# Cross-attention and FFN layer on one core: value product around the scores, input turned by VectorE through HBM, mask added on VectorE

## The reference, cut to what matters

```
xl    = layernorm(x)
q,k,v = xl @ Wq, ctx @ Wk, ctx @ Wv              # 512 -> 32 heads of 128
score = q.k / sqrt(128) + position_bias          # 16 x 32 x 64 x 64
score = where(mask, score, -inf); probs = softmax(score), 0 where not mask
x     = x + (probs @ v) @ Wo
out   = x + base(layernorm(x)) + lora(layernorm(x), router)
```

## Time and profile before

| | us |
|---|---|
| median of 3 runs | 779.62 |
| the runs | 779.62, 779.64, 775.87 |
| the profiled execution, its own time | 777.37 |
| span in its profile (first to last instruction) | 775.5 |
| PE busy | 766.0 |
| DVE busy | 541.8 |
| ACT busy | 384.8 |
| POOL busy | 196.6 |

### The profile page before, as it was taken

How to read it: one execution, slowest core, us unless ns; L and a number is a source line. 1 busy time by engine, 2 the same in 40 slices (tenths; PEclk the granted TensorE clock), 3 DMA queues, 4 the chain that set the end, 5 groups by cost and what they waited for, 6 DMA issues and landing times.

```text
span 775.5 us, 16682 instructions
## 1 busy us (share of the span) xinstructions
PE 766.0 (99%) x6272; PEld 639.1 (82%) x6272; DVE 541.8 (70%) x979; ACT 384.8 (50%) x1110; POOL 196.6 (25%) x203
## 2 busy tenths in 40 slices
PE   9999999999999999999999999999999999999998
PEld 7888888888888888887888888888888888888886
DVE  5874626257677676578778877887678767867974
ACT  5662526245555464475654465435543565426510
POOL 0224041014424433323132312232122313010300
PEclk9999999999999999999999999999999999999999
DMA  6536673244565456577766777556756666541002
GB/s 231 203 123 217 220 244 137 109 140 160 163 190 164 164 163 187 167 235 217 229 181 209 226 208 208 170 176 205 201 165 197 201 188 196 154 148 57 1 15 95
DMA packets 128236, 133.05 MB, mean 172 GB/s; under 512 B 46479, under 2 KB 93583, under 8 KB 128158
## 3 DMA queue, kind: packets, MB, share of 16 engines
q1 hardware_dynamic: 128158, 132.00, 54.3%
HBM read 88.98 MB, written 42.99 MB: 170 GB/s over the span
## 4 chain that ended last, share of the span: by engine, by line
PE 94%; DVE 3%; issue 1%; ACT 1%; DMA 0%; ACTq 0%
PE pY L1452 43%; PE pP L1452 40%; PE pY L1613 4%; PE pO L1649 2%; PE pT_ L1649 1%; PE pO L1452 1%; DVE y L1167 1%; ACT pr L798 1%; PE pS L1649 1%; DVE st L1018 1%; PE pO L1501 0%; PE pS L1501 0%; DVE wk_lo L948 0%; PE pY L1528 0%; DVE wo_lo L948 0%
## 5 line engine op out<-in xcount | busy, mean ns | idle before, releaser
L798 ACT ACTIVATE pr<-pr,mx 128x64 f32<-128x64 f32 x256 | 86.2, 343 | 68.0 <-DVE mx L1187 68.0
L1452 PE MATMUL pY<-wo_hi,oT_hi 128*128 128x512 f32 x248 | 97.3, 392 | 0.3 <-DVE y L1167 0.2
L1452 PE MATMUL pY<-wo_lo,oT_hi 128*128 128x512 f32 x248 | 96.6, 389 | 0.0
L1452 PE MATMUL pY<-wo_hi,oT_lo 128*128 128x512 f32 x248 | 96.5, 389 | 0.0
L1167 DVE TENSOR_TENSOR y<-y,pY 128x512 f32<-128x512 f32 x124 | 83.9, 676 | 15.2 <-PE pY L1452 14.1
L690 ACT CAST wk_hi<-twk 128x256 fp32r<-128x256 f32 x128 | 50.7, 408 | 65.2 <-PE pP L1452 53.4
L948 DVE TENSOR_TENSOR wk_lo<-wk_raw,wk_hi 128x256 fp32r<-128x256 f32 x96 | 48.5, 506 | 46.5 <-ACT wk_hi L690 45.1
L1452 PE MATMUL pP<-xo_hi,wk_hi 128*128 128x512 f32 x196 | 77.9, 398 | 0.0
L1452 PE MATMUL pP<-xo_lo,wk_hi 128*128 128x512 f32 x196 | 76.4, 390 | 0.0
L1452 PE MATMUL pP<-xo_hi,wk_lo 128*128 128x512 f32 x196 | 76.4, 390 | 0.0
L623 POOL TENSOR_TENSOR bias<-bias,madd 128x512 f32<-128x512 f32 x32 | 41.3, 1306 | 137.6 <-DMA bias<-in_fside_Bx32xSxS 137.5
(11 more groups left out here) (283 smaller groups left out, 1862.2 us busy)
## 6 DMA issues: line engine op xcount, KB each, us to landing
v_hbm<-stage SPq DMA_DIRECT2D x64, 256.0 KB, 2.1
k_hbm<-stage SPq DMA_DIRECT2D x64, 256.0 KB, 3.7
k<-k_hbm SPq DMA_DIRECT2D x16, 1024.0 KB, 6.4
v<-v_hbm SPq DMA_DIRECT2D x16, 1024.0 KB, 7.2
wk_raw<-in_L_xattn_Wk SPq DMA_DIRECT2D x16, 512.0 KB, 4.6
wo_raw<-in_L_xattn_Wo SPq DMA_DIRECT2D x16, 512.0 KB, 3.7
bias<-in_fside_Bx32xSxS SPq DMA_DIRECT2D x128, 64.0 KB, 3.6
wk_raw<-in_L_xattn_Wq SPq DMA_DIRECT2D x16, 512.0 KB, 4.6
```

Of the source, the lines that this page charges most:

```text
L798: nc.scalar.activation(pr[s][:, b, :], pr[s][:, b, :], ACT.Exp, bias=mx[:, s, b:b + 1], accum_out=sm[:, s, b:b + 1]).then_inc(exp_made, 1)
L1452: mm = nc.tensor.matmul(bank_, a, b, start=first and n == 0, stop=last and n == len(terms) - 1, skip_group_check=read_between)
```

## The change

The mask is no longer added to the bias by GpSimd; DVE adds it to the biased scores, as one more instruction between `biased` and `largest`. In the loop `times_v` of the first head goes ahead of both scores, and that of the second stays behind them. PE no longer turns x: DVE turns it in 32x32 blocks, SP writes each tile to HBM and reads it back across partitions in four DMAs (`x_out`, `x_back`), and ACT and DVE read the turned x from SBUF instead of PSUM; `rows_out` is not called for it. The moments and the normalising of x come one block earlier.

```diff
-FIRST_TURN = [0, 1, 4, 6, 8, 10, 12, 14]
+FIRST_TURN = [0, 1, 4, 6]
+            def x_out(j):
+                for i in range(2):
+                    sp.wait_ge(xb_made, 2 * j + i + 1)
+                    sp.dma_start(x_hbm[2 * j + i], xb[:, i, :, :].rearrange("p a n -> p (a n)")).then_inc(put_x[i], 16)
+            def x_back(j):
+                if j >= 1:
+                    sp.wait_ge(sum_step, 4 * (4 + j))
...
+                for i, dst in enumerate((first_x, low[1])):
+                    sp.wait_ge(put_x[i], 16 * (j + 1))
+                    blocks = x_hbm[2 * j + i].rearrange("(t k) (a n) -> a k t n", t=4, a=4)
+                    for a in range(4):
+                        sp.dma_start(dst[32 * a:32 * a + 32, :, :], blocks[a]).then_inc(ld_xt[i], 16)
...
                     load_wk(n - 10)
+                if 17 <= n < 29 and n % 3 == 2:
+                    x_out((n - 17) // 3)
                 if n != Q0:
                     store(n, 0, c11_made)
                 if 0 < n:
                     store(n - 1, 2, c21_made)
+                if 17 <= n < 29 and n % 3 == 2:
+                    x_back((n - 17) // 3)
...
-            def add_mask(h):
-                pool.wait_ge(ld_bias[h % 2], 64 * (h // 2 + 1))
-                b = bias[h % 2]
-                nc.gpsimd.tensor_tensor(b[:, :, :], b[:, :, :], madd[:, :, :], ALU.add).then_inc(bias_made, 1)
...
-                act.wait_ge(turned, FIRST_TURN[j] + 1)
+                if j < 4:
+                    act.wait_ge(turned, FIRST_TURN[j] + 1)
+                else:
+                    act.wait_ge(ld_xt[0], 64 * (j - 3))
...
+                for i in range(2):
+                    m = 2 * n + i
+                    dve.wait_ge(xn_made, m + 1)
+                    if n >= 1:
+                        dve.wait_ge(put_x[i], 16 * n)
+                    nc.vector.transpose(xb[:, i, :, :].rearrange("p g (c q) -> p c g q", c=DC),
+                                        xn[:, i, :].rearrange("p (c g q) -> p c g q", c=DC, g=4)).then_inc(xb_made, 1)
...
                 dve.wait_ge(s_full, h + 1)
-                dve.wait_ge(bias_made, h + 1)
+                dve.wait_ge(ld_bias[h % 2], 64 * (h // 2 + 1))
...
+                dve.wait_ge(s_read, h + 1)
+                dve.wait_ge(mask_made, 1)
+                nc.vector.tensor_tensor(pr[h % 2][:, :, :], pr[h % 2][:, :, :], madd[:, :, :], ALU.add
+                                        ).then_inc(masked, 1)
             def largest(h):
-                dve.wait_ge(s_read, h + 1)
+                dve.wait_ge(masked, h + 1)
...
-                if prep_at(n) is not None:
-                    turn_pair(prep_at(n))
...
                 if i == 0:
                     turn_p(h)
                     turn_p(h + 1)
-                scores(h + 2)
-                scores(h + 3)
-                times_v(h)
+                    scores(h + 2)
+                    scores(h + 3)
+                    times_v(h)
+                    times(n, 2)
+                else:
+                    times_v(h)
+                    scores(h + 2)
+                    scores(h + 3)
                 times_v(h + 1)
-                for p in (1, 2, 6, 7) if i else (2, 6, 7):
+                for p in (1, 2, 6, 7) if i else (6, 7):
                     times(n, p)
...
             h = 2 * i
+            times_v(h)
             scores(h + 2)
-            times_v(h)
             times_v(h + 1)
             scores(h + 3)
             ffn_weights(0)
```

More of the change, by code:

```diff
@@ L351, in raw_block, with first_of, second_of, like @@
             return raw[:, 2 * r:2 * r + 2, c * width:(c + 1) * width]
+        def first_of(j):
+            if j < 4:
+                return first_turn(j)[:, :].rearrange("p (c t) -> p c t", c=DC)
+            return first_x[:, :, :].rearrange("p t (c q) -> p c t q", c=DC)
+        def second_of(j):
+            if j < 4:
+                return second_turn(j)[:, :].rearrange("p (c t) -> p c t", c=DC)
+            return low[1][:, :, :].rearrange("p t (c q) -> p c t q", c=DC)
+        def like(j, a):
+            return a if j < 4 else a.rearrange("p c (t q) -> p c t q", t=4)
         def tw_of(w):
@@ L366, in tile_cols, with a01_of @@
             return slice(j % 4 * P, (j % 4 + 1) * P)
+        def a01_of(j, part):
+            return a_part(j, part)[:, 0:2, :, tile_cols(j)].rearrange("p k c t -> p (k c) t")
         def piece(n, i):
@@ L629, in _ @@
                     sums_of_b(wset(n + 1))
[L630 to L636, removed]
+                if 15 <= n < 27 and n % 3 == 0:
+                    rstd_of((n - 15) // 3 * 2)
+                    rstd_of((n - 15) // 3 * 2 + 1)
             for i in range(NP):
@@ L692, in first_high @@
             def first_high(j):
-                act.wait_ge(turned, FIRST_TURN[j] + 1)
-                nc.scalar.copy(a_part(j, 0)[:, 0:2, :, tile_cols(j)],
-                               first_turn(j)[:, :].rearrange("p (k c t) -> p k c t", k=2, c=2)).then_inc(a01_hi, 1)
+                if j < 4:
+                    act.wait_ge(turned, FIRST_TURN[j] + 1)
+                else:
+                    act.wait_ge(ld_xt[0], 64 * (j - 3))
+                nc.scalar.copy(like(j, a01_of(j, 0)), first_of(j)).then_inc(a01_hi, 1)
             def rows_out(j):
@@ L706, in last_high @@
             def last_high(j):
[L708 to L711, removed]
+                if j < 4:
+                    act.wait_ge(turned, SECOND_TURN[j] + 1)
+                else:
+                    act.wait_ge(ld_xt[1], 64 * (j - 3))
+                nc.scalar.copy(like(j, a_part(j, 0)[:, 6, :, tile_cols(j)]), second_of(j)[:, 2:4]).then_inc(a6_hi, 1)
             def sums_high(j):
@@ L778, in _ @@
                     first_high(j)
-                    rows_out(j)
                     last_high(j)
@@ L971, in first_low @@
             def first_low(j):
-                cols = tile_cols(j)
                 dve.wait_ge(a01_hi, j + 1)
-                lower(a_part(j, 1)[:, 0:2, :, cols], first_turn(j)[:, :].rearrange("p (k c t) -> p k c t", k=2, c=2),
-                      a_part(j, 0)[:, 0:2, :, cols], a01_lo)
+                lower(like(j, a01_of(j, 1)), first_of(j), like(j, a01_of(j, 0)), a01_lo)
             def last_low(j):
@@ L981, in last_low @@
                 dve.wait_ge(a6_hi, j + 1)
-                lower(a_part(j, 1)[:, 6, :, cols], second_turn(j)[:, 2 * P:4 * P].rearrange("p (c t) -> p c t", c=2),
-                      a_part(j, 0)[:, 6, :, cols], a6_lo)
+                lower(like(j, a_part(j, 1)[:, 6, :, cols]), second_of(j)[:, 2:4],
+                      like(j, a_part(j, 0)[:, 6, :, cols]), a6_lo)
             def sums_of_a(j):
-                low_, s, k = low[j // 4], sums_a[j // 4], SUM_ORDER.index(j)
-                one = first_turn(j)[:, :].rearrange("p (k c t) -> p k c t", k=2, c=2)
+                s, k = sums_a[j // 4], SUM_ORDER.index(j)
+                s2, s3, s1, s4 = (like(j, s[:, n, :, :]) for n in range(4))
                 if j == 0:
-                    one, low_ = kept0
+                    a11, a12 = kept0[0][:, 0, :, :], kept0[0][:, 1, :, :]
+                    rows_ = kept0[1][:, :, :]
                     dve.wait_ge(kept0_made, 2)
                 else:
-                    dve.wait_ge(low_made, k + 1 if j < 4 else k)
+                    a11, a12 = first_of(j)[:, 0:2], first_of(j)[:, 2:4]
+                    if j < 4:
+                        rows_ = low[0][:, :, :]
+                        dve.wait_ge(low_made, k + 1)
+                    else:
+                        rows_ = second_of(j)
+                        for i in range(2):
+                            dve.wait_ge(ld_xt[i], 64 * (j - 3))
                 if k >= 1:
                     dve.wait_ge(as_lo, k)
-                nc.vector.tensor_tensor(s[:, 2, :, :], low_[:, 0:2, :], low_[:, 2:4, :], ALU.add).then_inc(sum_step, 1)
+                nc.vector.tensor_tensor(s1, rows_[:, 0:2], rows_[:, 2:4], ALU.add).then_inc(sum_step, 1)
                 if j >= 3:
```

54 lines of the change are left out of this document (24 added, 30 removed).

## The result

The changed kernel takes 789.0 us (median of four runs, 788.6 to 789.6). A fourth run of the kernel before, 1092.43 us, is left out as a slow one. The forecast was 788 in a range of 778 to 795, slower: the time, the sign and the main mechanism came out as forecast, and some terms had the wrong size. The span grew from 775.5 to 787.2 us. PE's granted clock is 1.0, so no part of the loss is a matter of clock.

The account below looks back on a forecast made before the run. PE's own stream was taken to bound the kernel; -3.5 (x) + 0.8 (late loads) + 8.5 (passes) + 3.6 (three places) = +9.4 us, giving 786.8 profiled or 789 by the median; forecast 788, range 778 to 795.

Parts of the forecast that it names:

- main mechanism: Loop passes, p = 6 of the Q block: both delays exceed the cover, PE waits 0.9 us plus 0.1 restart.
- The term for the change of kind: Small products of a loop pass: one more switch between kinds of products lengthens PE's stream by 0.1 us (0 to 0.3).
- the cover holds: Rival, faster: first maximum under 0.9 us late, no wait at p = 6, halts end; some 774 us; chance 0.11.
- half of it: Rival, no change: a pass grows by only 0.5 us, level in total, 777 to 782 us; chance 0.14.
- loads late as well: Rival, slower still: PE waits 0.5 us for probabilities in some passes, x late four times; 793 to 799; chance 0.11.
- The halts: Thirteen loop passes: halt and new wait share a place and don't add up; together 335.1 us, 8.5 more.
- `add_tile(i, 0)`: Loop: without GpSimd's mask addition `lower_of(w, 1)` takes 0.42 us, the add costs PE nothing further; otherwise 0.5 us a pass.
- x: Blocks that turn x: four turns of 0.88 us leave PE, -3.5 us; late loads cost 0.8 us.
- the sign named beforehand: Sign of being right, at x: blocks 18, 21, 24 and 27 as long as their neighbours.
- The three places: Outside the thirteen passes: first scores 1.2 us, pass 0 0.7, after the last pass 1.7; together 3.6 us.
- The end: After the last pass: `times_wo(14, 3)` waits for `add_tile(14, 1)`, delayed by later scores and both additions; 1.7 us (0.7 to 2.5).
- Pass 0: Last `o_low` of pass 0: PE follows it with no cover, so its delay costs 0.7 us.

Follow-up runs that it names:

- order_only: Kernel before with only the order changed to V, scores, V (mask by GpSimd, x turned by PE): 779.9 us, ratio 1.0037.
- x_only: Kernel before with only x changed, turned by VectorE and through HBM: 774.6 us, ratio 0.9968.
- wide_v: x_only with the products with V made from 16 matmuls a head instead of 32: 795.3 us, ratio 1.0229.
- x_shift: x_only with 64 more small warming transposes at the start of PE's program: 775.3 us, ratio 0.9980.
- mask_only: Kernel before with only the mask addition moved to VectorE: 782.0 us, ratio 1.0056.
- act_order_x: Changed kernel with the mask back on GpSimd and ScalarE's two o_high ahead of exp(h + 2, 0) from pass 1 on: 778.4 us, ratio 1.0021.
- act_dve: act_first, and on VectorE make_c11 ahead of o_low(h, 1) and o_low(h + 1, 0) from pass 1 on: 780.9 us, ratio 1.0047.
- act_dve_c22: act_dve with make_c22 of block 32 ahead of the first pair's softmax instructions on VectorE: 778.9 us, ratio 1.0019.
- order_x: Changed kernel with the mask back on GpSimd, order and x as changed: 779.3 us, ratio 1.0027.
- act_first: Changed kernel with o_high(h, 0) and o_high(h, 1) ahead of exp(h + 2, 0) in ScalarE's queue from pass 1 on: 785.2 us, ratio 1.0112.
- mask_twice: Changed kernel with the mask addition done twice in a row on VectorE: 808.3 us, ratio 1.0410.

## Why the prediction was right, and where its sizes were off

**The main mechanism was right.** It said that the Q block hangs on the softmax through ACT's queue with a cover of 0.91 us, that one edit takes 0.72 and the other 1.1 of it, and that together they cost a wait of 0.9 and a restart of 0.1. Measured: 0.88 and 0.08. The mask alone left no wait at p = 6, the order alone 0.15; the forecast had "fit under" and "pass it by 0.2". Their sum in a pass is 0.53, together they cost 1.15, of which 0.15, 0.88 and 0.08 are accounted for. The term for the change of kind, 0.1, measured 0.15.

**The rival "the cover holds"** fell to the wait in the list, **"half of it"** to passes of 25.83, and **"loads late as well"** did not come about: `ld_p` was there 0.7 us or more ahead of each first value product of the loop, and no wait for it is listed.

**The halts.** The text argued that halt and wait share a place and don't add up, and put the thirteen passes at 335.1. They took 336.64: eleven passes nearly as forecast (25.83 against 25.78, 0.6 us in all), and two with a halt that is longer than the wait that it replaces (0.9 us). This term is the largest that was mis-sized, by 1.5 us.

**`add_tile(i, 0)`** was right: the slow `lower_of(w, 1)` is 0.43 us in the changed kernel, 0.92 in order_only, where GpSimd still adds the mask, and nothing in the loop waits for the add.

**x.** Forecast -2.7 (-3.5 and 0.8 of late loads); measured -2.3 from block 14 to block 28 in the changed kernel and -2.7 in x_only. The turning blocks were 0.93, 0.89, 0.93 and 0.89 us longer than their neighbours, not 0.88. Loads were late in two of the four: blocks 21 and 27 remain 0.31 and 0.85 us longer in the changed kernel, so that the sign named beforehand, these blocks as long as their neighbours, held for 18 and 24 alone (0.07). In block 27 it looks like this, in ACT's row and PE's:

```profile
275.67 0.41 ACT L751 CAST xo_hi<-low_x 128x256 fp32r<-128x256 f32 x1 [1.27 <-DMA low_x<-x_hbm]
```

```profile
276.70 0.47 PE L1506 MATMUL pY<-co_hi,wk_hi 128*128 128x512 f32 x1 [0.56 <-ACT u_s L706]
```

That is the chain named in the forecast, `copy_u` and then p = 5, though `last_high` is late and not `first_high`.

**The three places.** Block 32: 1.2 forecast, 1.4 measured. The end: 1.7 and 1.7, but in another place: 0.8 of it is a wait at 712.68, where `times_wo(14, 0)` follows the last `o_low` (that ends at 712.57), and `times_wo(14, 3)`, at which the forecast had put it all, waits 0.4. That the size is right is partly luck. Pass 0: 0.7 and 1.0. There the step overlooked `make_c11`, which stands behind four softmax instructions and two additions: p = 7 waits for it first, the last `o_low` only afterwards.

**The sum** was +9.4. By PE's last instruction it is +12.1 (771.98 and 784.06): 1.5 in the passes, 0.7 at x (0.3 of it from the start-up), 0.5 at the three places. That the forecast of 788 lies 1 us from the median is therefore partly luck: it was made against a before of some 778.6 (788 less 9.4), while the recorded ratio goes with 777.2, and what the sum lacks is nearly made up by that.

## What to carry to other kernels

When a stream without waits is changed, look for its nearest cover: how long a result lies ready before it is used, and what stands in the same queue ahead of it. Two delays that each fit under the cover, or nearly, don't fit together, so a change of several parts is worth running part by part: here the part that gained 2.5 us was hidden under two that cost 4.4 and 2.9 alone and some 7 more together. What has to wait for a late result should not stand ahead of what has not; moving two copies on ACT and one addition on DVE gave 8 us back without any work less.

## What the runs showed of the hardware

The halts of PE without releaser hang on its instruction stream. The trace shows an instruction queue whose packets of 16 KB come nine in four passes; it is PE's, as there are 50 of them in the changed kernel and 42 in wide_v, which differs on PE in having fewer matmuls. In the fourteen kernels of this study (before and after among them) every halt inside the small products of the loop (more than 0.2 us from one start to the next) ended 2.1 to 2.9 us after the start of such a packet. The times in the expectation of x_shift are these too; the halts begin anywhere from 0.4 to 2.7 us after that start, so that it is the end that hangs on the packet:

```
kernel      passes with a halt          us from packet to end of halt
before      3, 4, 7, 8, 11              2.32 to 2.88
mask_only   3, 4, 7, 8, 11              2.25 to 2.77
x_only      0, 1, 4, 5, 8, 12, 13       2.15 to 2.73
x_shift     2, 3, 6, 10, 14             2.43 to 2.74
after       4, 5, 8, 12                 2.39 to 2.71
wide_v      none
```

The mask alone leaves PE's program as it was, and its halts stand in the same passes as those of before. 32 transposes fewer moved them one pass later, 64 more moved them two passes earlier, and half as many, slower matmuls in the products with V ended them. Long waits go with short halts. Eight kernels have the same matmuls on PE, in one of two orders: x_only, act_order_x, act_dve and act_dve_c22 with next to no wait at p = 6 and 7 (halts of 5.8, 5.1, 3.2 and 2.3 us), order_x with 0.15 us in a pass (2.7), act_first with 0.4 (0.9), after with 0.9 (0.9) and mask_twice with 1.9 (0.1). So a wait of PE near a dense run can cost less than it shows, and taking it away can give less back; by how much, one execution of each doesn't tell, since the halts differ by 3 us among the kernels that have no such wait. Why some packets come late and others not was not settled. The Trainium skill (Runtime: NRT & Kernel Launch, Instruction fetch mechanics) says that instructions come in blocks of 16 KiB, 256 of them, and that crossing such a boundary is mostly hidden. The first agrees: 283 matmuls and 283 weight loads a pass make 252 for each of nine packets in four passes. The second doesn't hold in a run of 64x64 matmuls, where up to 2.0 us were lost at one boundary.

Two more were unexpected. A matmul that waits so briefly that it still overlaps the one before is named in no list of waits, but costs its delay and 0.08 us of restart; only start-to-start times show it. And fewer, wider matmuls were slower: the two heads' products take 2.03 us as 64 matmuls of 64 columns, and 1.71 us more as 32 of 128.
